# Summing part of every message bucket during the filter layer of a two-layer graph network

## What is computed

```python
edge_index = jnp.stack([src, dst])          # idx_i = src, idx_j = dst
h = x @ w_in + b_in                                        # (12500, 64)
Wij = (ssp(f_ij @ w_f1 + b_f1) @ w_f2 + b_f2) * rcut_ij[:, None]
agg = jax.ops.segment_sum(h[idx_j] * Wij, idx_i, n_atoms)  # (12500, 64)
x = _layernorm(x + ssp(agg @ w_o1 + b_o1) @ w_o2 + b_o2)
deg = segment_sum(ones, dst); dinv = rsqrt(deg)
msg = (x @ W)[src] * (dinv[src] * dinv[dst])[:, None]
out = segment_sum(msg, dst) + b      # then a norm over nodes, relu
return _layernorm(x + out)
```

## Time and profile before

| | us |
|---|---|
| median of 3 runs (7589.79 to 7602.98) | 7600.19 |
| the profiled execution, its own time | 7595.02 |
| its span, first to last instruction | 7593.3 |
| filter stages, first to last scatter | 226.3 to 4506.5 |
| bucket stage, first load to last fold | 4507.8 to 5025.7 |
| granted TensorE clock, mean of the span | 0.768 |

### The profile page before, as it was taken

How to read it: one execution, slowest core, us unless ns; L and a number is a source line. 1 busy time by engine, 2 the same in 40 slices (tenths; PEclk the granted TensorE clock), 3 DMA queues, 4 the chain that set the end, 5 groups by cost and what they waited for, 6 DMA issues and landing times. The chain is left out here.

```text
span 7593.3 us, 149535 instructions
## 1 busy us (share of the span) xinstructions
PE 5875.8 (77%) x41800; PEld 4237.4 (56%) x41800; DVE 5172.3 (68%) x13223; ACT 3579.3 (47%) x5657; POOL 5129.2 (68%) x5181
## 2 busy tenths in 40 slices
PE   7777767777776777777777757766899999999994
PEld 6555555555555555555555546654566666666662
...
PEclk5676666766667676666666669986999999999995
...
GB/s 127 80 84 83 83 81 68 55 55 54 56 55 55 55 55 56 55 55 55 55 55 56 55 119 353 356 192 141 91 76 76 76 77 76 76 77 76 76 77 74
DMA packets 442124, 679.58 MB, mean 89 GB/s; under 512 B 222677, under 2 KB 322607, under 8 KB 428593
## 3 DMA queue, kind: packets, MB, share of 16 engines
...
## 5 line engine op out<-in xcount | busy, mean ns | idle before, releaser
L1499 POOL DMA_INDIRECT msg_tab<-big x3224 | 3239.6, 1005 | 1076.8 <-issue 1076.8
L2039 POOL DMA_INDIRECT big<-y_parts,big x1616 | 1589.7, 984 | 550.9 <-issue 490.3
L2120 ACT CAST big<-ps 128x980 bf16<-128x980 f32 x804 | 784.3, 976 | 1275.9 <-PE ps L2068 1273.3
L2080 PE MATMUL ps<-big 128*128 128x384 bf16 x6566 | 1196.9, 325 | 0.2 <-ACT big L2120 0.2
L2172 DVE TENSOR_SCALAR big<-big,dstF 128x343 bf16<-128x343 f16 (+2 forms) x3216 | 978.0, 336 | 220.8 <-PE ps L2068 220.4
L1341 DVE TENSOR_TENSOR big<-big 128x512 f32<-128x512 f32 x403 | 279.2, 693 | 1211.3 <-ACT big L1236 1211.3
L1236 ACT CAST big<-big 128x512 bf16<-128x512 f32 x403 | 249.2, 618 | 1660.3 <-DMA msg_tab<-big 1660.1
L1057 PE MATMUL ps<-big 128*128 128x128 f32 x3224 | 763.1, 411 | 306.7 <-ACT big L1231 306.7
L1057 PEld LDWEIGHTS ps<-big 128*128 128x128 f32 x3224 | 648.5, 298 | 578.8 <-ACT big L1231 578.8
L2080 PEld LDWEIGHTS ps<-big 128*128 128x128 bf16 x6566 | 580.7, 97 | 348.8 <-issue 1.9
L1049 PE MATMUL ps<-big 2*128 2x512 bf16 x806 | 318.2, 483 | 558.7 <-ACT big L1220 558.7
...
## 6 DMA issues: line engine op xcount, KB each, us to landing
...
big<-in_edge_attr SPq DMA_DIRECT2D x403, 128.0 KB
...
big<-h_parts SPq DMA_DIRECT2D x403, 48.0 KB
...
```

The costliest lines, as they stand in the source:

```text
L1499: nc.gpsimd.indirect_dma_start(out=m.msg_tab[:, :], out_offset=bass.IndirectOffsetOnAxis(ap=sidx[s][:, j:j + 1], axis=0), in_=row[s][:, j, ...
L2039: nc.gpsimd.indirect_dma_start(out=m.grow[s][:, 3 * D * j:3 * D * j + 3 * D], out_offset=None, in_=m.y_parts[:, :], in_offset=bass.Indirec ...
L2080: mm = pe.matmul(ps_rows, m.cnt[h][:, a, :], m.y_part[:, HALF * h + a, :], start=(h == 0 and a == 0), stop=(h == 1 and a == HALF - 1))
L2120: nc.scalar.copy(m.cnt[h][:, :, SLOTS * i:SLOTS * i + SLOTS].rearrange("p h (a w) -> p h a w", a=2), ps_cnt[i % 2][:, :, 0:SIDE * HALF].re ...
```

## The change

Of the 36 parts of a bucket (97 of the 98 buckets), the first 13 are loaded and summed in filter stages 201 to 298, one bucket a stage, and the next 8 in stages 299 to 396. Each is a *segment*. In such a stage SP issues one more load (645 KB, later 397 KB) and one more store (32 KB); PE adds 13 (8) more products at the head of its stage (`sum_seg`); DVE folds the sum of the segment before with three small operations (`fold_seg`), and at its end copies the low digits and makes the 13 (8) one-hot tiles (`hot_seg`). The folded sums go to a new table `agg_parts` in DRAM. The last stage loads the other 15 parts (728 KB) and the two earlier sums (64 KB) of each bucket, and POOL makes four additions for a bucket where it made two. Bucket 97 is loaded and summed whole, as before. The segment buffers lie in the first 5858 columns of `x`, so ACT loads these columns again (2.9 MB) at the start of the bucket stage. The table of node numbers is written before the first filter stage and copied at the start of the bucket stage. The setup counts the buckets a third time, and tests that after 6 and 9 of its 13 counting steps every bucket has its first 1664 and 2688 rows; if not, the general path runs instead. The diff, cut to its core:

```diff
@@ -79,8 +79,14 @@
...
 PUT = (4 + LAST) // 2
-EARLY = 6
+EARLY, LATER = 6, 9
+SEG = (13, 8)
+SEG_AT = (0, 13 * P)
+REST_AT = sum(SEG) * P
+REST = BT - sum(SEG)
+SEG_FROM = (201, 299)
 WIDE = 112
+X_USED = 5858
 MROW = 3 * F + 2
...
@@ -163,6 +169,7 @@
...
         self.agg_sum = nc.dram_tensor("agg_sum", [NT, F], F32)
+        self.agg_parts = nc.dram_tensor("agg_parts", [NBK * P, 2 * F], F32)
         self.msg_tab = nc.dram_tensor("msg_tab", [NBK * BROWS, MROW], BF16)
...
@@ -771,6 +781,51 @@
...
         body(b, b % 3, b // 3)
+def bucket_rows(b):
+    return BT if isinstance(b, int) and b == NBK - 1 else REST
+def slot_of(part, here):
+    return (here[1] - SEG_FROM[part[0]]) % 2
+def staged_parts(eng, n, stage):
+    def near(g):
+        return [(k, k % 2, k // 2) if 0 <= k < n else None for k in (g - 1, g, g + 1)]
+    def part(g):
+        for phase, at in enumerate(SEG_FROM):
+            if at <= g <= at + NBK - 1:
+                return phase, g - at
+        return None
+    def loop(a, z):
+        with eng.Fori(0, (z - a) // 2) as i:
+            for c in (a, a + 1):
+                at = part(a)
+                stage(*[(2 * i + k, k % 2, i + k // 2) for k in (c - 1, c, c + 1)],
+                      (at[0], 2 * i + c - SEG_FROM[at[0]]) if at else None)
+    def alone(g):
+        stage(*near(g), part(g))
+    alone(-1)
+    alone(0)
+    loop(1, SEG_FROM[0])
+    alone(SEG_FROM[0])
+    loop(SEG_FROM[0] + 1, SEG_FROM[0] + NBK - 1)
+    alone(SEG_FROM[0] + NBK - 1)
+    alone(SEG_FROM[1])
+    loop(SEG_FROM[1] + 1, SEG_FROM[1] + NBK - 1)
+    alone(SEG_FROM[1] + NBK - 1)
+    loop(SEG_FROM[1] + NBK, n - 2)
+    for g in (n - 2, n - 1, n):
+        alone(g)
...
@@ -937,9 +1008,53 @@
...
                     zero_hole(2 * i + s)
-            with sp.Fori(NBK // 2 - 1, (G - 3) // 2) as i:
+            def load_seg(phase, k, s):
+                q = (NBK - 1) * phase + k
+                if phase == 1 and isinstance(k, int) and k == 0:
+                    sp.wait_ge(seg_summed, NBK)
+                if not isinstance(k, int) or k >= 2:
+                    sp.wait_ge(seg_summed, q)
+                sp.sem_inc(window_turn, 1)
+                n = SEG[phase]
+                sp.dma_start(seg[s].rearrange("p r c -> p (r c)")[:, 0:n * MROW],
+                             m.msg_tab[bass.ds(k * BROWS + SEG_AT[phase], n * P), :].rearrange("(p r) c -> p (r c)", p=P)
+                             ).then_inc(seg_in[s], 16)
+            def store_seg(phase, k, s):
+                sp.wait_ge(seg_folded, (NBK - 1) * phase + k + 2)
+                sp.sem_inc(window_turn, 1)
+                sp.dma_start(m.agg_parts[bass.ds(k * P, P), F * phase:F * phase + F], seg_agg[s]).then_inc(parts_out[s], 16)
+            def turn_alone(k):
+                turn(k, k % 2)
+                for phase, at in enumerate(SEG_FROM):
+                    if 0 <= k - 4 - at < NBK - 1:
+                        store_seg(phase, k - 4 - at, (k - at) % 2)
+                for phase, at in enumerate(SEG_FROM):
+                    if k == at + 1 and phase == 0:
+                        for s in range(2):
+                            sp.wait_ge(scattered[s], 64 * EARLY * HG + 16 * PUT)
+                    if k == at + 1 and phase == 1:
+                        for s in range(2):
+                            sp.wait_ge(scattered[s], 64 * LATER * HG + 16 * PUT)
+                    if 0 <= k - 1 - at < NBK - 1:
+                        load_seg(phase, k - 1 - at, (k - 1 - at) % 2)
+            with sp.Fori(NBK // 2 - 1, SEG_FROM[0] // 2) as i:
                 for s in range(2):
                     turn(2 * i + s + 2, s)
+            done = 2 * (SEG_FROM[0] // 2) + 2
+            for phase, at in enumerate(SEG_FROM):
+                for k in range(done, at + 4):
+                    turn_alone(k)
+                with sp.Fori(0, (NBK - 4) // 2) as i:
+                    for c in (4, 5):
+                        turn(2 * i + at + c, (at + c) % 2)
+                        store_seg(phase, 2 * i + c - 4, c % 2)
+                        load_seg(phase, 2 * i + c - 1, (c - 1) % 2)
+                done = at + NBK
+            for k in range(done, G - 1):
+                turn_alone(k)
             sp.wait_ge(dst_out, G - 2)
...
@@ -953,9 +1068,19 @@
...
+            for s in range(2):
+                sp.wait_ge(parts_out[s], 16 * (NBK - s))
             def load_bucket(b, t):
-                sp.dma_start(bucket[t].rearrange("p r c -> p (r c)"),
-                             m.msg_tab[bass.ds(b * BROWS, BROWS), :].rearrange("(p r) c -> p (r c)", p=P)).then_inc(bucket_in[t], 16)
+                if isinstance(b, int) and b == NBK - 1:
+                    sp.dma_start(bucket[t].rearrange("p r c -> p (r c)"),
+                                 m.msg_tab[b * BROWS:(b + 1) * BROWS, :].rearrange("(p r) c -> p (r c)", p=P)).then_inc(bucket_in[t], 16)
+                    return
+                sp.dma_start(bucket[t].rearrange("p r c -> p (r c)")[:, 0:REST * MROW],
+                             m.msg_tab[bass.ds(b * BROWS + REST_AT, REST * P), :].rearrange("(p r) c -> p (r c)", p=P)).then_inc(bucket_in[t], 16)
+            def load_parts(b, t):
+                sp.dma_start(before_rest[t], m.agg_parts[bass.ds(b * P, P), :]).then_inc(parts_in[t], 16)
...
@@ -968,9 +1093,12 @@
...
                 store_agg(b, t)
+                if not isinstance(b, int):
+                    load_parts(b + 3, t)
...
                 load_bucket(t, t)
+                load_parts(t, t)
             with sp.Fori(0, (NBK - 3) // 3) as i:
...
@@ -979,6 +1107,8 @@
...
                 store_agg(b, b % 3)
+                if b + 3 < NBK - 1:
+                    load_parts(b + 3, b % 3)
             for t in range(3):
...
@@ -1089,7 +1219,19 @@
...
-            def stage(before, here, after):
+            def sum_seg(phase, k, s):
+                q = (NBK - 1) * phase + k
+                n = SEG[phase]
+                pe.wait_ge(seg_hots, q + 2)
+                pe.wait_ge(seg_folded, q + 1)
+                hots = seg_hot[:, 0:P * n].rearrange("p (n r) -> p n r", r=n)
+                for r in range(n):
+                    mm = pe.matmul(ps_seg, hots[:, :, r], seg[s][:, r, 0:3 * F], start=(r == 0), stop=(r == n - 1))
+                mm.then_inc(seg_summed, 1)
+            def stage(before, here, after, part):
+                if part and not (isinstance(part[1], int) and part[1] == 0):
+                    sum_seg(part[0], part[1] - 1, slot_of(part, here) ^ 1)
                 if after:
...
@@ -1109,13 +1251,16 @@
...
             pe.wait_ge(tables_put, 4)
-            staged(pe, G, stage)
+            pe.sem_inc(seg_summed, 1)
+            staged_parts(pe, G, stage)
...
                 pe.wait_ge(sums_out, b + 1)
-                for r in range(BT):
-                    mm = pe.matmul(ps_bucket[t], node_hot[t][:, :, r], bucket[t][:, r, 0:3 * F], start=(r == 0), stop=(r == BT - 1))
+                n = bucket_rows(b)
+                hots = node_hot[t][:, 0:P * n].rearrange("p (n r) -> p n r", r=n)
+                for r in range(n):
+                    mm = pe.matmul(ps_bucket[t], hots[:, :, r], bucket[t][:, r, 0:3 * F], start=(r == 0), stop=(r == n - 1))
                 mm.then_inc(bucket_summed, 1)
...
@@ -1244,12 +1389,17 @@
...
             staged(act, G, stage)
+            act.wait_ge(seg_folded, 2 * (NBK - 1) + 1)
+            act.wait_ge(tables_put, 6)
+            for a, z in ((0, WIDE), (WIDE, NP)):
+                act.dma_start(m.xs_flat[a:z, 0:X_USED], io["x"].rearrange("(p c) d -> p (c d)", p=NP)[a:z, 0:X_USED]).then_inc(x_back, 16)
...
             thirds(act, copy_sums)
+            act.wait_ge(x_back, 32)
...
@@ -1359,11 +1509,41 @@
...
-            def stage(before, here, after):
+            def fold_seg(phase, k, s):
+                q = (NBK - 1) * phase + k
+                dve.wait_ge(seg_summed, q + 2)
+                dve.sem_inc(seg_seen, 1)
+                nc.vector.tensor_copy(seg_small, ps_seg[:, 2 * F:3 * F]).then_inc(seg_halves, 1)
+                dve.wait_ge(seg_halves, 2 * q + 1)
+                nc.vector.tensor_tensor(seg_small, seg_small, ps_seg[:, F:2 * F], ALU.add).then_inc(seg_halves, 1)
+                dve.wait_ge(seg_halves, 2 * q + 2)
+                dve.wait_ge(parts_out[s], part_stores(phase, s, k))
+                nc.vector.tensor_tensor(seg_agg[s], seg_small, ps_seg[:, 0:F], ALU.add).then_inc(seg_folded, 1)
+            def hot_seg(phase, k, s):
+                q = (NBK - 1) * phase + k
+                n = SEG[phase]
+                dve.wait_ge(seg_in[s], seg_loads(phase, s, k))
+                dve.wait_ge(seg_hots, q + 1)
+                nc.vector.tensor_copy(seg_low[:, 0:n], seg[s][:, 0:n, 3 * F]).then_inc(seg_lows, 1)
+                dve.wait_ge(seg_lows, q + 1)
+                dve.wait_ge(seg_summed, q + 1)
```

(41 more changed lines are left out.)

55 lines of the change are left out of this document (37 added, 18 removed).

## The result

The changed kernel takes 7508.57 us (median of 4 runs, 7498.46 to 7511.49) against 7599.43 us; the ratio is 0.988 with a 95% interval of 0.9863 to 0.9897. It is 91 us faster, where 139 were forecast; 7508 lies within the range given and in the forecast's own range, near the high end. Of the forecast gain 65% came.

The account below looks back on a forecast made before the run. POOL's scatters bound the filter stages, DMA reading buckets the bucket stage. From 7595, minus 203 (bucket stage) plus 65 (filter stages) gives 7457, stated as 7460; the forecast's own range 7400 to 7520, the whole range 7375 to 7565.

Parts of the forecast that it names:

- The port: Filter stages: two-input DVE one-hots make POOL's scatters wait, 0.32 us a stage for 13 parts, 0.12 for 8.
- Rival 4: Filter stages: the one-hots don't stretch POOL's scatters; 43 us less, 7417; chance 0.05.
- The new loop: Filter stages, 13 parts: one-hots to one-hots through PE, DVE and ACT takes 10.75 us, 0.13 over POOL's 10.62.
- rival 1: Filter stages: the PE and DVE loop sets the stage at low clock, 11.5 and 10.9 us; 7519; chance 0.11.
- Transfers in the filter stages: Filter stages: segment loads add 61 GB/s, DMA share 0.20 to about 0.4, and cost nothing.
- Rival 5: Filter stages: segment loads delay the scatters' landing beyond 4.3 us of slack; at 6 us, 7728; chance 0.03.
- The chain from fold to fold: Bucket stage: load, one-hots, products, additions and SP's queue sum to 12.1 us over four buckets, 3.0 each.
- the price of the products: Bucket stage: PE's 15 products for a bucket at 0.10 us each, 1.5 us in the chain.
- Rival 3: Bucket stage: TensorE at half clock, products take 3.0 us, a bucket 3.37; 36 us more, 7496; chance 0.06.
- The reload: Bucket stage: loading 2.9 MB of `x` again on ACT's queue costs 5 us, bounds 0 and 8.5.
- Rival 2: Bucket stage: POOL's four additions set 3.75 us a bucket; 72 us more, 7532; chance 0.07.
- rival 6: Setup: the tests of the bucket counts fail and the general path runs, slower by far; chance 0.01.

Follow-up runs that it names:

- the second trace: The changed kernel run and profiled once more, unaltered, on the chip of three other kernels: 7496.2 us, ratio 0.9877 to the kernel before.
- the reduction: Changed kernel with a segment's one-hot operation in the filter stages replaced by a one-input reduction of about the same length, early sums left out: 7477.0 us, ratio 0.9857.
- two experiments: Changed kernel with bucket-stage stores and earlier-sum loads on ACT's queue, 7462.4 us (0.9842); separately, with two POOL additions a bucket for four, 7462.9 us (0.984).

## Why the prediction was right or wrong, point by point

- *What bounds the kernel.* Right. POOL's scatters still set the filter stages, and the bucket stage was the place to gain.
- *The port.* Right in kind. Scatters that begin under the one-hots are longer by 0.25 us a stage with 13 parts (0.34 in the second trace) and 0.11 (0.13) with 8, where 0.32 and 0.12 were taken. But the scatters as a whole gained 0.5 and 0.27 a stage. The forecast counted the new operation alone; the changed stage also lets more scatters begin under L1498, which it didn't price. That the two numbers for the one-hots fit is in part luck: they were taken at 0.92 and 0.57 us and are 1.09 and 0.69, with which the formula gives 0.45 and 0.18. The Trainium skill's inference (SBUF — State Buffer, "Who interferes with whom") that `tensor_tensor` doesn't hold up descriptor generation disagrees with the traces here: scatters under the two-input operation take 1.31 us on average, those under a reduction of the same length 0.97. Rival 4 is out.
- *The new loop.* Forecast at 10.1 to 11.2, taken as 10.75. It lies near 11.0: the reduction left the stage at 10.97. The forecast took 10.75 because PE would come nearer to its dense state, where the clock is 0.9 and more; PE was busy 82% and the clock stayed at 0.68. Of that, rival 1 was right about the low clock, though POOL waited for nobody in the window of 13 parts, so the loop was only close behind. The two limits don't add; the longer one counts, so 0.13 for a loop over 10.62 on top of the port was the wrong kind of sum. The steps that were right: the path through products, attributes, hidden layer, ranks and one-hots, confirmed by moving one operation by 0.7 us. What the forecast didn't see is that DVE's fold holds up the stage as soon as the products come later.
- *Filter stages in sum.* 65 forecast, 78.5 measured: 98 x 0.51 with 13 parts, 98 x 0.25 with 8, 2.4 before the first scatter, and 1 to 2 us elsewhere.
- *Transfers in the filter stages.* Right: 114 GB/s instead of 55 at a DMA share of 0.38, and L1381 still waits for its scatter 98 us in 1000 us of 13-part stages (2380 to 3380) without POOL waiting for what follows. Rival 5 didn't occur.
- *The chain from fold to fold.* Right, and the main gain rests on it: two experiments moved the spacing by what the chain says. Its size was off: 3.0 forecast, 3.43 measured, over four buckets 1.6 us. Followed link by link in the trace, from the fold of bucket b to that of b + 4 for 82 buckets, the means are: fold to load 1.66, load to landing 4.81, digits 0.23, one-hots 1.24, products 2.27, ACT's copy 0.32, additions with their gaps 2.39, and hand-overs 0.73. That is 13.65 us, and the forecast had 12.1.
- *The term that missed most* is the price of the products, 2.27 us in place of 1.5. "264.9 us for 2664 products is 0.10 each" was read at a granted clock near 0.9 and carried over to a stage in which PE is busy 65% and the clock is 0.67. The other misses are the landing (4.81 in place of 4.3), SP's three instructions (1.66 in place of 1.2) and the one-hots; the additions are 0.3 shorter than forecast. As the run with added products shows, not all of the 0.77 would come back with the clock. Rival 3 had this mechanism with a chance of 0.06 and a spacing of 3.37, close to the 3.43 that came; but its price of 36 us isn't borne out, since bringing the clock back gave 5 to 7, net of the added products. The Trainium skill (TensorE: Matmul & The Clock Gate, "HAM oscillation — how this bites in real kernels") describes short bursts between waits that bring the clock down; the 0.67 here and the 0.98 of the run that filled the waits agree in direction. There the waits are longer than the bursts; here bursts of 1.5 to 2.6 us stand between waits of about 1.1 us at the median.
- *The reload.* 5 us forecast, 8.5 as the bound, 10 to 12 measured. The bound took the bytes alone; the loads of SP behind it come late, and the chain carries that on.
- *Rival 2* (POOL's throughput) and *rival 6* (the general path) are out: POOL is busy half of the time, and the general path didn't run.
- *The sum.* Bucket stage 315 forecast, 358.9 measured; of the difference of 44, 96 x 0.43 = 41 is the spacing and the rest the reload. With the 13.5 us of the filter stages, less the 3.3 that the part behind the bucket stage is shorter, that is the distance from 7457 to 7511.5. The measured 7508.57 is nearer to the times of rival 1 (7519) and rival 3 (7496) than to the forecast's 7460; the forecast's mechanisms held, and its range was wide enough for sums that were too low in both stages.
